# A causal-window attention block on one core: the eight blocks of queries in the order 0, 7, 2, 6, 1, 5, 3, 4 instead of 0 to 7

## The reference, cut to what matters

```
h = silu(x @ W1.T + b1) @ W2.T + b2
q, k, v = split(h @ Wg.T + bg)            # 16 heads of 64
dots = q @ k.T * 64 ** -0.5
dots = where(j >= i + 64, -inf, dots)      # query i sees keys 0 .. i + 63
out = softmax(dots) @ v                    # per head
return out @ Wo.T + bo
```

## Time and profile before

| | us |
|---|---|
| median of three runs | 1462.04 |
| the profiled execution, its own time | 1458.82 |
| span of its instructions | 1457.0 |
| busy: PE / GpSimd / VectorE / ScalarE | 1354.4 / 1043.7 / 881.5 / 819.7 |
| one turn of the loop | 40.14 |

### The profile page before, as it was taken

The page is one execution under the profiler, slowest core; times in us unless marked ns, Lnnn a source line. Parts: engine busy times, 40 slices in busy tenths (PEclk is TensorE's granted clock), DMA queues, the critical chain, the costliest instruction groups (busy, mean ns, idle before and its releaser), DMA issues.

```text
span 1457.0 us, 32231 instructions
## 1 busy us (share of the span) xinstructions
PE 1354.4 (93%) x10770; PEld 998.9 (69%) x10770; DVE 881.5 (61%) x1726; ACT 819.7 (56%) x1789; POOL 1043.7 (72%) x656
## 2 busy tenths in 40 slices
PE   5979999999999999999999999999999999999888
PEld 4846666667776666667767676676677776666667
DVE  5746666655666666565565665666665666566545
ACT  2536565555566556555556565565555556556532
POOL 7737777777777777777777777777777777777763
PEclk9989999999999999999999999999999999999999
DMA  3100000000000000000000000000000000000001
GB/s 107 41 0 22 21 21 20 20 20 20 16 4 20 20 20 20 20 20 20 20 20 0 20 20 20 20 20 20 20 20 20 14 6 20 20 20 0 1 8 52
DMA packets 31358, 29.45 MB, mean 20 GB/s; under 512 B 7009, under 2 KB 26338, under 8 KB 31330
## 3 DMA queue, kind: packets, MB, share of 16 engines
q1 hardware_dynamic: 31330, 29.09, 6.6%
HBM read 8.07 MB, written 2.10 MB: 7 GB/s over the span
## 4 chain that ended last, share of the span: by engine, by line
PE 83%; ACT 6%; issue 6%; DVE 4%; DMA 1%; ACTq 0%; POOL 0%; SPq 0%; DVEq 0%; POOLq 0%
PE banks L831 21%; PE banks L813 21%; PE banks L794 19%; PE banks L718 6%; ACT probs L438 5%; PE banks L780 4%; PE banks L696 3%; DVE negmax L571 3%; PE banks L722 2%; PE banks L772 2%; PE banks L688 2%; PE banks L689 2%; PE banks L678 1%; DMA xres<-in_x 1%; ACT probst L446 0%
## 5 line engine op out<-in xcount | busy, mean ns | idle before, releaser
L368 POOL TENSOR_SCALAR probs<-probs,recips 128x704 f32<-128x704 f32 (+7 forms) x512 | 948.8, 1866 | 347.2 <-DVE recips L576 345.0
L571 DVE TENSOR_REDUCE negmax<-banks 128x1 f32<-128x704 f32 (+7 forms) x512 | 393.4, 810 | 199.9 <-PE banks L794 194.9
L446 ACT ACTIVATE probst<-banks 128x512 f32<-128x512 f32 (+1 forms) x416 | 241.3, 580 | 432.4 <-PE banks L813 428.7
L438 ACT ACTIVATE probs<-banks,negmax 128x704 f32<-128x704 f32 (+7 forms) x512 | 399.1, 786 | 13.1 <-DVE negmax L571 10.6
L813 PE MATMUL banks<-ident,probs 128*128 128x128 f32 x2752 | 386.4, 279 | 3.4 <-ACT probst L446 1.8
L813 PEld LDWEIGHTS banks<-ident,probs 128*128 128x128 f32 x2752 | 297.9, 141 | 66.1 <-issue 55.6
L831 PE MATMUL banks<-probst,vs 128*64 128x256 f32 (+1 forms) x2944 | 325.5, 370 | 0.9 <-DVE probst L583 0.9
L583 DVE COPY probst<-banks 128x512 f32<-128x512 f32 (+1 forms) x320 | 202.2, 632 | 181.4 <-PE banks L813 181.4
L794 PE MATMUL banks<-kt,qt 64*128 64x512 f32 (+4 forms) x2496 | 298.1, 364 | 3.0 <-issue 3.0
L831 PEld LDWEIGHTS banks<-probst,vs 128*64 128x64 f32 x2944 | 200.2, 137 | 126.7 <-issue 35.4
L794 PEld LDWEIGHTS banks<-kt,qt 64*128 64x128 f32 x2496 | 205.9, 185 | 50.1 <-issue 5.7
(11 more groups left out here) (59 smaller groups left out, 782.7 us busy)
## 6 DMA issues: line engine op xcount, KB each, us to landing
hslot<-h_sb SPq DMA_DIRECT2D x32, 512.0 KB, 3.3
wslot<-in_wqkvt SPq DMA_DIRECT2D x32, 128.0 KB, 2.9
wslot<-wq_sb SPq DMA_DIRECT2D x32, 64.0 KB, 2.6
y<-xres SPq DMA_DIRECT2D x8, 256.0 KB, 2.3
xres<-in_x SPq DMA_DIRECT2D x2, 256.0 KB, 3.8
wo_sb<-in_wot SPq DMA_DIRECT2D x1, 512.0 KB
wq_sb<-in_wqkvt SPq DMA_DIRECT2D x1, 512.0 KB
bslot<-bqk_sb SPq DMA_DIRECT2D x32, 1.0 KB, 1.9
```

The source lines that it names most:

```text
L368: nc.gpsimd.tensor_scalar(here, here, recips[:, c, h:h + 1], None, ALU.mult).then_inc(normed.sem, 1)
L438: nc.scalar.activation(probs[c, h][:, 0:width[c]], src, ACT.Exp, bias=negmax[:, c, h:h + 1], accum_out=sums[:, c, h:h + 1]).then_inc(exped ...
L446: nc.scalar.activation(probst[c // 2 % 2][:, 4 * g:4 * g + w, c % 2 * P:(c % 2 + 1) * P], banks[:, TRANSPOSED[g % 2], 0:w * P].rearrange(" ...
L571: nc.vector.tensor_reduce(negmax[:, c, h:h + 1], src, AX.X, ALU.max, negate=True).then_inc(maxed.sem, 1)
```

## The change

The step `c` no longer works on the block of queries `c` but on `at_step[c]`, the list 0, 7, 2, 6, 1, 5, 3, 4. The widths by step are then 192, 1024, 448, 960, 320, 832, 576 and 704. The pairs whose values are multiplied together are the blocks (0, 7), (2, 6), (1, 5) and (3, 4). Lags, `ATTEND_AT` and `OUTPUTS` are as they were (the latter is written in another order). The projections move: `v0` and `v1` to steps 1 and 2, and `k0`, `k1`, `q0`, `q1` of the next turn to steps 3 to 6, so that steps 0 and 7 have none; before, steps 1 and 7 had none. Turn 0 gets `k0`, `k1` and `q0` ahead of the attention in three banks, and `q1` after them in bank 4, once `k0` has been read. The residual is added to two blocks that are no longer neighbours, through a strided view. The work after the last turn is written for the five steps that are still owed.

```
--- before.py
+++ after.py
@@ -49,8 +49,10 @@
     assert D == P and N == 1024 and CH == BANK
 
     STEPS = N // P
-    width = [min(c * P + P + WINDOW, N) for c in range(STEPS)]
+    at_step = [0, 7, 2, 6, 1, 5, 3, 4]
+    width = [min(q * P + P + WINDOW, N) for q in at_step]
     blocks = [-(-w // P) for w in width]
     groups = [-(-2 * n // 4) for n in blocks]
     T_LAG, PV_LAG = 3, 5
@@ -62,10 +64,10 @@
 
     ATTEND_AT = {5: 0, 7: 1, 1: 2, 3: 3}
 
-
-    OUTPUTS = {0: "o1", 2: "o2", 4: "o3", 6: "o0"}
-    JOBS = {0: "k1", 2: "q1", 3: "v0", 4: "v1", 5: "k0", 6: "q0"}
-    FIRST = (("k0", 5), ("q0", 6))
+    OUTPUTS = {6: "o0", 0: "o1", 2: "o2", 4: "o3"}
+
+    JOBS = {1: "v0", 2: "v1", 3: "k0", 4: "k1", 5: "q0", 6: "q1"}
+    FIRST = (("k0", 4), ("k1", 5), ("q0", 6))
     JOB_ORDER = list(JOBS.values())
 
 
@@ -75,7 +77,7 @@
 
     def mask_pieces(c):
 
-        lo, hi = c * P + WINDOW, width[c]
+        lo, hi = at_step[c] * P + WINDOW, width[c]
         cuts = [lo] + [b for b in (BANK,) if lo < b < hi] + [hi]
         return [(a // BANK, a % BANK, a - lo, b - a) for a, b in zip(cuts, cuts[1:])]
 
@@ -189,9 +191,9 @@
                  T("taken_vector", [(c, g) for c in range(STEPS) for g in range(1, groups[c], 2)])]
         attended = T("attended", range(STEPS // 2))
         attn_out = T("attn_out", range(STEPS // 2))
-        proj = T("proj", ["k0", "q0", "k1", "q1", "v0", "v1"])
-        qk_high = T("qk_high", ["k0", "q0", "k1", "q1"])
-        qk_done = T("qk_done", ["k0", "q0", "k1", "q1"])
+        proj = T("proj", ["k0", "k1", "q0", "q1", "v0", "v1"])
+        qk_high = T("qk_high", ["k0", "k1", "q0", "q1"])
+        qk_done = T("qk_done", ["k0", "k1", "q0", "q1"])
         v_done = T("v_done", ["v0", "v1"])
         wo_done = T("wo_done", ["o0", "o1", "o2", "o3"])
         wo_added = T("wo_added", ["o0", "o1", "o2", "o3"])
@@ -241,10 +243,10 @@
 
         def job_turn(job, i):
 
-            return i + 1 if job in ("k0", "q0") else i - 1 if job in ("o1", "o2", "o3") else i
+            return i + 1 if job[0] in "kq" else i - 1 if job in ("o1", "o2", "o3") else i
 
         def runs(job, carry, more):
-            return more if job in ("k0", "q0") else carry or job not in ("o1", "o2", "o3")
+            return more if job[0] in "kq" else carry or job not in ("o1", "o2", "o3")
 
         block = ctx.enter_context(nc.Block())
 
@@ -467,6 +469,7 @@
                 if job[0] in "kq" and runs(job, carry, more):
                     queries_keys(job, job_turn(job, i), 1 - r if job_turn(job, 0) else r)
 
+            queries_keys("q1", 0, 0, 4)
             for c in range(STEPS):
                 step(c, 0, 0, carry=False)
             with act.Fori(0, TURNS // 2 - 1) as i2:
@@ -476,12 +479,13 @@
                     step(c, i2 * 2 + 2, 0)
             for c in range(STEPS):
                 step(c, TURNS - 1, 1, more=False)
-            for c in range(STEPS - T_LAG, STEPS):
-                take(c, 0, TURNS - 1)
-                if groups[c] > 2:
-                    take(c, 2, TURNS - 1)
-                if c >= STEPS - 2:
-                    attention_out(c - STEPS + 4, TURNS - 1)
+            for c in range(PV_LAG):
+                if c < T_LAG:
+                    take(c + STEPS - T_LAG, 0, TURNS - 1)
+                    if groups[c + STEPS - T_LAG] > 2:
+                        take(c + STEPS - T_LAG, 2, TURNS - 1)
+                if c in ATTEND_AT:
+                    attention_out(ATTEND_AT[c], TURNS - 1)
 
             feed_forward(pd)
 
@@ -600,12 +604,13 @@
             def add_output(name, i):
 
                 j = int(name[1])
-                at = (i // PAIRS) * N + j * 2 * P
+                first, second = at_step[2 * j:2 * j + 2]
+                at = (i // PAIRS) * STEPS + first
                 at = at if isinstance(at, int) else dve.snap(at)
                 dve.wait_ge(wo_done.sem, wo_done.after(name, i))
                 dve.wait_ge(wo_added.sem, wo_added.after(name, i - 1))
-                here = xres[:, bass.ds(at, 2 * P)]
-                nc.vector.tensor_tensor(here, banks[:, ATTEND, 2 * P:4 * P], here, ALU.add).then_inc(wo_added.sem, 1)
+                here = xres[:].rearrange("p (k d) -> p k d", d=P)[:, bass.ds(at, 2, step=second - first), :]
+                nc.vector.tensor_tensor(here, banks[:, ATTEND, 2 * P:4 * P].rearrange("p (k d) -> p k d", d=P), here, ALU.add).then_inc(wo_added.sem, 1)
 
             def evict(job, i, r, carry, more):
 
@@ -640,6 +645,7 @@
 
             for name, bank in FIRST:
                 queries_keys_low(name, 0, 0, bank)
+            queries_keys_low("q1", 0, 0, 4)
             for c in range(STEPS):
                 step(c, 0, 0, carry=False)
             with dve.Fori(0, TURNS // 2 - 1) as i2:
@@ -651,11 +657,13 @@
                 step(c, TURNS - 1, 1, more=False)
             for t in range(3):
                 statistics(pd, "ln1", t)
-            for c in range(STEPS - T_LAG, STEPS):
-                take(c, 1, TURNS - 1)
-                if groups[c] > 3:
-                    take(c, 3, TURNS - 1)
-                add_output(f"o{c - STEPS + 4}", TURNS - 1)
+            for c in range(PV_LAG):
+                if c < T_LAG:
+                    take(c + STEPS - T_LAG, 1, TURNS - 1)
+                    if groups[c + STEPS - T_LAG] > 3:
+                        take(c + STEPS - T_LAG, 3, TURNS - 1)
+                if c in OUTPUTS:
+                    add_output(OUTPUTS[c], TURNS - 1)
             dve.wait_ge(wo_added.sem, wo_added.after("o3", TURNS - 1))
 
             feed_forward(pd)
@@ -782,16 +790,14 @@
             def score(c, i, r):
 
                 masked = {b for b, _, _, _ in mask_pieces(c)}
-
-                needs = {0: "q0", 3: "k1", 4: "q1"}
-                if c in needs:
-                    pe.wait_ge(qk_done.sem, qk_done.after(needs[c], i))
+                if c < 2:
+                    pe.wait_ge(qk_done.sem, qk_done.after(("q0", "q1")[c], i))
                 edges = list(range(0, width[c], BANK)) + [width[c]]
                 for b, (a, z) in enumerate(zip(edges, edges[1:])):
                     terms = ((0, 0), (0, 1), (1, 0))
                     for n, (sq, sk) in enumerate(terms):
                         for h in range(2):
-                            last = mm(banks[:, SCORE[h] + b, 0:z - a], qt[r][sq][half(h), c * P:(c + 1) * P], kt[r][sk][half(h), a:z],
+                            last = mm(banks[:, SCORE[h] + b, 0:z - a], qt[r][sq][half(h), at_step[c] * P:(at_step[c] + 1) * P], kt[r][sk][half(h), a:z],
                                       start=n == 0 and b not in masked, stop=n == 2, skip_group_check=True)
                             if z == width[c] and n == 2:
                                 last.then_inc(scored.sem, 1)
@@ -816,9 +822,8 @@
 
             def attend(p, i, r):
 
-                if p < 2:
-
-                    pe.wait_ge(v_done.sem, v_done.after("v0" if p == 0 else "v1", i))
+                if p == 0:
+                    pe.wait_ge(v_done.sem, v_done.after("v1", i))
                 pe.wait_ge(attn_out.sem, attn_out.after(*last_pair(i, p)))
                 q, t = last_pair(i, p)
                 pe.wait_ge(wo_added.sem, wo_added.after(f"o{q}", t))
@@ -865,6 +870,8 @@
             pe.wait_ge(pa.h.sem, pa.h.after("h", CHUNKS - 1))
             pe.wait_ge(pa.x1.sem, pa.x1.after("x", CHUNKS - 1))
             pe.wait_ge(zeroed, 2 * sum(width[c] < blocks[c] * P for c in range(STEPS)))
+            pe.wait_ge(qk_done.sem, qk_done.after("k0", 0))
+            project("q1", 0, 0, 4)
             masks(0, 0)
             for c in range(STEPS):
                 step(c, 0, 0, carry=False)
@@ -875,12 +882,13 @@
                     step(c, i2 * 2 + 2, 0)
             for c in range(STEPS):
                 step(c, TURNS - 1, 1, more=False, final=True)
-            for c in range(STEPS - T_LAG, STEPS):
-                turns_of(c, TURNS - 1, (0, 1, 2, 3))
-                p = c - STEPS + 4
-                if p > 1:
-                    attend(p, TURNS - 1, 1)
-                output(f"o{p}", TURNS - 1)
+            for c in range(PV_LAG):
+                if c < T_LAG:
+                    turns_of(c + STEPS - T_LAG, TURNS - 1, (0, 1, 2, 3))
+                if c in ATTEND_AT:
+                    attend(ATTEND_AT[c], TURNS - 1, 1)
+                if c in OUTPUTS:
+                    output(OUTPUTS[c], TURNS - 1)
 
             pe.wait_ge(wo_added.sem, wo_added.after("o3", TURNS - 1))
             feed_forward(pd)
```

## The result

The changed kernel takes 1391.97 us (median of 4 runs, 1390.04 to 1393.28), the kernel before beside it 1460.71 us: ratio 0.9523, 95% interval 0.9511 to 0.9535. That is 4.8% faster. The profiled execution took 1391.63 us with a span of 1389.7, against 1458.82 and 1457.0. Where one run of a kernel lies far above its others (one of e8's four, 3050.88 us), it is left out.

A forecast was written before the change was run, and what follows sets the result against it. PE was taken to bound most of the kernel, the score cycle the wide steps. Loop -55, start and turn 0 +6, turn 31 -4, after it -3.5: -56.5 from 1458.8 gives 1402.3, median 1405 us; range 1394 to 1432.

The forecast's parts named there:

- score cycle: Each step's chain of mask, scores, row maximum, exponentials, next mask; no lag hides it; 4.35 to 5.52 us in steps 4 to 7.
- the price of a product: Products with the values: columns are paid, not records; 0.108 us a wide record, 0.056 a half one.
- GpSimd's queue: GpSimd's work a turn stays 29.65 us, and three steps cover its queue.
- the sum of steps: Each step of a turn takes the longer of PE's work and the score cycle; 38.3 us in sum.
- Rivals B and C: Weight loads price half records: B 0.082 each, 1445 us, chance 0.05; C 0.109 each, slower, 1485 us, chance 0.05.
- Rival A: Row maxima queue behind copies in four steps, 0.3 us each: 1.2 a turn, 1443 us; chance 0.20.
- D: Stalls at PE's changeovers in steps 1, 4 and 6 buy the balance back: 1455 to 1466 us, chance 0.04.
- 1.85 us less a turn, 55 us in the 30 turns of the loop: The loop's gain, from the steps' prices and cycles before and after the change.
- 40.14: Length in us of one loop turn before the change, read from the trace; the priced steps gave 40.06.
- 38.3: Forecast length in us of a loop turn after the change, summed over its eight steps.
- a value projection 1.15: PE's price in us for v0 or v1, used in steps 1 and 2 of the new turn.
- My added wait: Steps 4 to 7: row maxima queue behind projection copies, lengthening the cycles by 1.1, 0.4, 0.6 and 0.5 us.

The follow-up runs named there:

- e8: Changed kernel with another alternation of blocks, 0, 4, 1, 5, 2, 6, 3, 7: 1411.19 us, 0.9660 of the kernel before.
- e1: Changed kernel with the new places of the projections but the blocks in old order 0 to 7: 1464.74 us, 1.0029 of the kernel before.
- e3: Changed kernel with every 256-wide product of values split into two 128-wide ones (only its time is read): 1474.22 us, 1.0076 of the kernel before.
- e2: Changed kernel with each projection one step earlier, in steps 0 to 5: 1411.07 us, 0.9652 of the kernel before.
- e10: Changed kernel with only the products of blocks 3 and 4 split, from their second 128 keys on: 1392.86 us, 0.9539 of the kernel before.
- e6: Kernel before, with q1's rest taken from the projection's bank ahead of the residual's addition in step 2: 1453.79 us, 0.9951 of the kernel before.
- e4: Changed kernel with the output of step 4 put ahead of that step's projection: 1381.96 us, 0.9461 of the kernel before.
- e5: Changed kernel with blocks 1 and 2 swapped, order 0, 7, 1, 6, 2, 5, 3, 4: 1383.73 us, 0.9463 of the kernel before.
- e7: Changed kernel with both e4's earlier output and e5's swapped blocks: 1381.96 us, 0.9463 of the kernel before.
- e9: Changed kernel with all wide products split from their second 128 keys on: 1470.77 us, 1.0073 of the kernel before.

## Why the prediction was right, and where it was wrong

**Right.** That the score cycle of the wide blocks was the idle time and that alternating the widths hides it (e1); that the price of a product goes by columns (2.32, 2.53, 2.32, 2.75 us against 2.33, 2.52, 2.34, 2.76 foretold, and e3's 48 records in 2.77); that GpSimd's queue has room (PE has no wait for it in the loop); that the total is near the sum of steps, each the longer of PE's work and its cycle (e2 and e8 fell inside the ranges told in advance, though the chain of e2's step 6 is another than the cycle). The 81 ns a matmul that the Trainium skill (TensorE: Matmul & The Clock Gate, Back-to-back issue gap) gives for 128 columns does not describe these pairs of column halves: e3's 48 records of 128 columns take 2.77 us, 58 ns each, and e10's 16 more records a turn cost less than can be measured. Rivals B and C fell with it. Rival A did not happen here, D neither.

**Wrong in size**, by its own terms (us, differences of the chain's rows; the forecast behind each). The rows of after are these:

```profile
140.07 0.22 PE banks L788 x2
...
1281.06 0.22 PE banks L788 x2
...
1315.92 0.17 DVE recips L580
...
1332.44 0.67 PE banks L686 x4
...
1335.67 0.43 PE banks L697
```

| | before | after | difference | forecast |
|---|---|---|---|---|
| up to the start of turn 1 | 132.23 | 140.07 | +7.8 | +6 |
| 30 turns of the loop | 1208.35 | 1140.99 | -67.4 | -55 |
| turn 31 | 40.25 | 34.86 | -5.4 | -4 |
| up to the last feed-forward phase | 20.42 | 16.52 | -3.9 | -3.5 |
| the last phase | 55.75 | 57.26 | +1.5 | 0 |

So the step that failed is "1.85 us less a turn, 55 us in the 30 turns of the loop", which measured 2.25 and 67.4; the other rows add up to 1.5 us the other way. The forecast then put the median 3.2 us above the profiled execution. It is 1.9 above it before and 0.3 after, so this term holds 2.9 of the 13 us between 1405 and 1392. The loop's error has two parts.

*The turn before was not 40.14.* That was one turn. (1340.58 - 132.23) / 30 from the earlier trace rows, which I had in hand, gives 40.28. Every second turn is about 0.3 us longer, in step 0, where the loop branches back (start, length, line of the kernel before):

```profile
776.66 0.27 PE banks L780 x2
776.93 0.20 issue
777.13 0.58 PE banks L794 x6
```

After, a pair of turns differs by 0.17 only. This is 4.2 us.

*The turn after was not 38.3 but 38.03*, 8 us. The term that failed is "a value projection 1.15": it is 0.89, and the remaining 0.23 to 0.26 were PE's wait for q1 to leave the projection's bank. That wait was in the profile before (6.9 us in all), and e6 takes it out of the kernel before for 7 us. Two such projections make 0.52 us a turn. Other terms give back some 0.2 of it (step 0 took 0.12 more, the last two tiles of step 1 took 0.37 for 0.22), and every second turn is longer by 0.17.

Two terms were right by luck. In step 4 I had PE reach the projection's bank when it is free, "nothing", and took 4.3 for the score cycle. In fact PE waits there, and its work with this wait makes 4.29; e4 shows it. The weight load for this projection in the timeline after:

```profile
731.04 0.30 PEld L726 LDWEIGHTS banks<-hslot,wslot 128*128 128x128 f32 x2 [0.21 <-DVE kt L595]
```

The projection takes 1.10 behind this wait of 0.21, and 0.86 in steps 3, 5 and 6. In step 6 I took 4.6 for the cycle, but the chain has PE alone: the scores of width 576 cost 1.15, not the 1.01 of the line between two widths, as they are twelve records where 448 keys take six. My added wait therefore set no step. Its 1.85 was also read too freely: in the earlier trace rows the copy ends at 727.48, and the maximum starts when its own scores end, at 727.54 in the chain. Step 0, taken at its cycle of 2.85, is PE's work alone too (2.97, as its mask took 0.22 and its last six tiles 0.78, where I had 0.11 and 0.65).

The range was too narrow below: 0.2 us a turn for the prices, when a single price, used twice, carried 0.5, and nothing for the turn taken as the mean. The last phase's +1.5 is the clock: from 1335.3 to 1338.6 us its granted value is 0.50, the lower of the two levels, and matmuls take 0.43 each where they took 0.24 before. The profiled executions of e4, e5 and e7 have 0.23 to 0.24 there, e4's clock at 1.00. I have no cause for when it falls.

The start cost 7.8 where I had 6: the first mask of turn 0 comes at 101.08, 3.9 us later than before, where I had 1.6 and counted `q1`'s 1.5 into turn 0. Turn 0 itself takes 38.99 (39.5 foretold).

## What to carry to other kernels

Where a chain inside a step cannot be overlapped with itself, list for each step the chain's length and the bound engine's other work, and reorder the steps so that no step's chain is the longer; the total of work says nothing about it. Take a price from the cleanest place where it occurs and look for a wait in front of it, and take a loop's turn as an average over many turns. When the engine is at last busy all through, a wait of 0.2 us a turn is worth a look: the output ahead of the projection in one step brought 10 us more, 8.5 of them in the loop (e4, 1382 us, with e7 the fastest here).

## What I had not expected of the hardware

A loop whose program grows past an edge pays on every pass: between 1522 and 1618 trace records of PE a pass, the instruction queue goes from 17 transfers in all to 144, and the passes that were read have a pause of 3.2 to 3.6 us in step 0, with a spell at the lower clock behind it, 79 to 82 us in all (e9, e3). In e9's trace the loop makes nine transfers a pass; in the trace of e10 it makes none from 230 to 1281 us. That the number of records is what counts is argued from these runs: they also differ in which products are split. The changed kernel, with 1458 records, is some 60 to 160 records short of this. The Trainium skill (Runtime: NRT & Kernel Launch, Instruction fetch mechanics) speaks of blocks of 16 KiB (256 instructions), a store of 128 KiB for TensorE (2048 instructions) and a stall when a branch's target lies outside a window of two blocks. The transfers here are of that block size (2.36 MB in 144). A window of two blocks, 512 instructions, does not fit the trace: e10's pass has 814 records without the matmuls, and fetches nothing. The edge was not placed more closely.

The branch back also costs more where PE is waiting at the end of the loop. Where step 7 ends on the score cycle, every second turn is longer by 0.3 (before) or 0.5 us (e1: 780.43 - 740.27 = 40.16, the next 40.63; e8: 38.42 and 38.90). Where PE is late there, step 0 behind the branch is longer by 0.1 only (after, 3.08 against 2.97; e4, 3.08 against 2.98); the rest of the 0.17 in the kernel after is the wait in step 4. The branch's own record stands 0.07 us behind the mask of the new turn in the trace before (776.73), with the next matmul 0.40 later; after, it stands 0.35 us ahead of that mask (748.25), while the product of step 7 still runs. So PE's instruction stream is then past the branch before the array is out of work. That this alone makes the difference was not tested by a run.
